# Attention heads: the division ahead of the first marking, three blocks of turned scores at the head of TensorE's round, the first scores ahead of the sample

## The reference, cut to what matters

```python
draft = jnp.einsum('bhqd,bhkd->bhqk', qr, kr)
draft = draft + jnp.where(causal_future, neg, 0.0)
_, draft_indices = jax.lax.top_k(draft, num_remain)      # the 128 largest of each row
mask = mask.at[b_idx, h_idx, s_idx, draft_indices].set(0.0)
mask = jnp.where(causal_future[None, None, :, :], neg, mask)
scores = jnp.einsum('bhqd,bhkd->bhqk', qr, kr) / np.sqrt(HD) + mask
attn = jax.nn.softmax(scores, axis=-1)
out = jnp.einsum('bhqk,bhkd->bhqd', attn, v)
```

## Time and profile before

| | |
|---|---|
| median of 3 runs | 3335.14 us (3334.58 to 3335.22) |
| the profiled execution | 3335.86 us |
| its span | 3334.0 us |
| busy share of the span: PE, DVE, ACT, POOL | 89%, 74%, 60%, 50% |
| mean granted TensorE clock over the span | 0.908 of full speed |
| the stage of the attention heads | from about 2060 to 3215 us |
| granted clock in that stage | 0.76 |

### The profile page before, as it was taken

How to read it: one execution, slowest core, us unless ns; L and a number is a source line. 1 busy time by engine, 2 the same in 40 slices (tenths; PEclk the granted TensorE clock), 3 DMA queues, 4 the chain that set the end, 5 groups by cost and what they waited for, 6 DMA issues and landing times. The chain is left out here.

```text
span 3334.0 us, 50391 instructions
## 1 busy us (share of the span) xinstructions
PE 2975.7 (89%) x15823; PEld 1814.0 (54%) x15929; DVE 2472.3 (74%) x4628; ACT 1987.7 (60%) x4218; POOL 1653.5 (50%) x3659
## 2 busy tenths in 40 slices
PE   8999999999999999999999897488888888788769
PEld 4455454464554544645545444266666666666654
DVE  5677696796876967968769767677777777777646
ACT  2463564554545645545456235888888888888723
POOL 3245264262452642634526446766666666666503
PEclk9999999999999999999999998577777777777889
DMA  2122132131221321312213100000000000000010
GB/s 91 57 87 85 69 112 89 63 111 70 86 86 70 111 90 61 111 70 86 86 57 111 56 26 2 1 1 1 2 2 1 2 1 1 1 1 1 2 49 26
DMA packets 65803, 169.62 MB, mean 51 GB/s; under 512 B 11776, under 2 KB 19328, under 8 KB 64512
## 3 DMA queue, kind: packets, MB, share of 16 engines
q1 hardware_dynamic: 54448, 115.17, 10.7%
q10 hardware_dynamic: 11088, 51.19, 4.4%
HBM read 161.08 MB, written 5.24 MB: 50 GB/s over the span
## 5 line engine op out<-in xcount | busy, mean ns | idle before, releaser
L2052 ACT ACTIVATE X<-ah_z,ah_trial 128x256 bf16<-128x256 f32 (+6 forms) x896 | 732.8, 824 | 25.2 <-POOL ah_trial L2155 14.1
L1207 ACT ACTIVATE m_mix<-m_mix,m_cs 128x128 f32<-128x128 f32 x1024 | 312.9, 388 | 256.6 <-DMA m_mix<-cs_rows 256.6
L2007 PE MATMUL ah_ps_o<-a_v,X 128*128 128x17 f32 x2304 | 353.9, 282 | 44.6 <-DVE hT L2252 44.6
L2007 PEld LDWEIGHTS ah_ps_o<-a_v,X 128*128 128x128 f32 x2304 | 338.6, 220 | 51.9 <-ACT X L2063 49.8
L2063 ACT ACTIVATE X<-ah_ps_e 128x512 f32<-128x512 f32 (+3 forms) x384 | 186.4, 486 | 192.5 <-PE ah_ps_e L1994 129.2
L2224 DVE TENSOR_SCALAR_CACHE_REDUCE X<-ah_z,ah_cut 128x256 bf16<-128x256 f32 (+6 forms) x224 | 193.7, 875 | 128.9 <-POOL ah_cut L2160 128.9
L1089 POOL TENSOR_TENSOR m_xdec<-m_xdt,m_decay_out 128x512 f32<-128x512 f32 x112 | 142.6, 1273 | 213.2 <-DVE m_xdt L1333 202.1
L1117 POOL TENSOR_TENSOR m_squares<-m_squares 128x256 f32<-128x256 f32 x128 | 107.4, 839 | 273.7 <-ACT m_squares L1219 273.7
L2237 DVE MAX8 ah_top<-ah_ps_m 128x8 f32<-128x256 f32 (+6 forms) x224 | 186.0, 830 | 69.1 <-PE ah_ps_m L1957 61.8
L1013 PE MATMUL m_ps_x<-m_w_out,m_gate 128*128 128x512 f32 x512 | 233.8, 599 | 0.0
L1013 PE MATMUL m_ps_d<-m_w_out,m_gate 128*128 128x512 f32 x512 | 233.5, 599 | 0.0
(11 more groups left out here) (319 smaller groups left out, 7782.0 us busy)
## 6 DMA issues: line engine op xcount, KB each, us to landing
m_mix<-cs_rows SPq DMA_DIRECT2D x128, 512.0 KB, 4.4
m_w_proj<-in_w_proj ACTq DMA_DIRECT2D x69, 512.0 KB, 3.3
m_fade<-fade_rows SPq DMA_DIRECT2D x224, 128.0 KB, 2.9
m_w_out<-in_w_out ACTq DMA_DIRECT2D x7, 2048.0 KB, 8.0
X<-in_x SPq DMA_DIRECT2D x8, 256.0 KB, 4.9
m_w_out<-in_w_out SPq DMA_DIRECT2D x1, 2048.0 KB, 10.1
x_away<-X SPq DMA_DIRECT2D x1, 2048.0 KB, 7.3
X<-x_away SPq DMA_DIRECT2D x8, 256.0 KB, 5.9
```

What stands on the lines that cost most here:

```text
L1207: act.activation(mix[:, u % 3, h, :], mix[:, u % 3, h, :], ACT.Relu, bias=cs[:, c, h0 + h:h0 + h + 1], scale=-1.0).then_inc(lag_done, 1)
L2007: last = pe.matmul(ps_o[:, t, :], eT[:, g % 3, b * P:(b + 1) * P], v[:, b0 + b, h // REP, :], start=i == 0 and b == 0, stop=b0 + b == t, s ...
L2052: act.activation(sign[:, at % 2, 0:(t + 1) * P], z[:, h % RING, cols(t)], ACT.Sign, bias=trial[:, h % RING, 0, t - 1:t], scale=-1.0, accum ...
```

## The change

Three things are moved, and no instruction is added or removed:

1. On PE, chunk 2 goes from behind the scores of tile 1 to the head of the round. Every later chunk but the last goes one place forward. Chunk 10, which stood between the marked scores and the scores of tile 7, now stands behind the scores of tile 6, and nothing takes its place.
2. On DVE, `divide(n - 4)` goes from behind tile 1 of the picking loop to a place ahead of `take(n - 2, 1)`.
3. On PE and DVE, the scores of tile 0 and their evacuation go ahead of the sample.

```diff
-    CHUNKS_FIRST = (0, 1)
-    CHUNKS_AFTER_MARKED = ((), (), (), (), (), (6,), (8,), (10,))
-    CHUNKS_AFTER_SCORES = ((), (2,), (3,), (4,), (5,), (7,), (9,), (11,))
+    CHUNKS_FIRST = (0, 1, 2)
+    CHUNKS_AFTER_MARKED = ((), (), (), (), (), (7,), (9,), ())
+    CHUNKS_AFTER_SCORES = ((), (3,), (4,), (5,), (6,), (8,), (10,), (11,))
@@ PE @@
                 if live(n + 1):
+                    scores(n + 1, 0)
                     sample(n + 1)
-                    scores(n + 1, 0)
@@ DVE @@
                 if live(n + 1):
+                    evacuate(n + 1, 0)
                     sample(n + 1)
-                    evacuate(n + 1, 0)
                     add_sample(n + 1)
+                if live(n - 4):
+                    divide(n - 4)
                 if live(n - 2):
                     take(n - 2, 1)
                     take(n - 2, 2)
@@
-                    if t == 1 and live(n - 4):
-                        divide(n - 4)
```

## The result

The changed kernel takes 3255.5 us (median of 4 runs, 3250.62 to 3258.75) against 3335.18 us before (4 runs). The ratio is 0.976 with a 95% interval of 0.9743 to 0.9777: 80 us less, inside the range of 3213 to 3305 and 5.5 us above the forecast of 3250. The profiled execution took 3250.62 us, with a span of 3248.7 us; it is the fastest of the four.

The account below looks back on a forecast made before the run. It took a loop of waits through ACT, POOL's cut, DVE and PE to bound the kernel. 27 rounds x (34.18 - 31.2) = 80.5 us plus 4.4 for the last three rounds gave 3250 us, range 3213 to 3305.

Parts of the forecast that it names:

- The loop before: Old round of 34.6 us: 19.95 from `take` to ACT's chunk 7, 9.44 on ACT, 5.2 through POOL's cut to `take`.
- The division in DVE's idle time: Division fits DVE's 3.44 us idle before `take`, removing PE's 1.48 us stop and 0.49 us of DVE's chain.
- The chunks: Chunks earlier on PE: chunk 7 ready 15.1 to 15.8 us after `take` instead of 19.95; ACT's waits nearly vanish.
- The new loop: DVE's chain from `take` to tile 7, then PE's head and the division: 29.9 to 32.9 us, taken as 31.2.
- Tile 0 ahead of the sample: One matmul pair on PE goes ahead of the sample's wait for ACT's `row_out`: worth 0 to 0.2 us, taken as 0.
- The clock: PE's slow stretch at the head shrinks from 10 us to some 4, the middle one stays; granted clock over 0.8.
- The sum: 27 rounds x (34.18 - 31.2) = 80.5 us, plus 4.4 for the last three rounds with picks: 85 us less.
- A full clock: First rival: PE's clock stays full once its gaps are filled, round 29.9 us, 3215 us; chance 0.12.
- Today's clock: Rival: PE's clock stays slow at the same places, round 32.9 to 33.1 us, 3300 us; chance 0.15.
- The slower side: Rival: `take` waiting for the division makes the round 35.7 us, 41 us more in all, 3376 us; chance 0.08.
- the new tie: `take` of tile 1 can't start before chunk 11 is added: 3.35 to 4.15 us behind tile 7's evacuation.
- No effect: Rival: the loop runs through another link, POOL's first move, so nothing changes, 3335 us; chance 0.03.

Follow-up runs that it names:

- warm16: The changed kernel with 16 extra matmuls in PE's gap ahead of tile 0's scores, their result overwritten: 3220.63 us.
- takes_ahead: divide_tables with the division moved behind the takes of tiles 1 and 2, ahead of the first pick: 3248.89 us.
- divide_tables: The changed kernel with the sample put back ahead of tile 0 on PE and DVE; division and chunk tables stay moved: 3243.39 us.
- divide_only: The kernel before with only the division moved ahead of the takes: 3285.49 us.
- chunk0_takes_ahead: chunk0_first with the division moved behind the takes of tiles 1 and 2: 3235.06 us.
- chunk0_first: divide_tables with chunk 0 and `add_v` of chunk 10 moved ahead of tile 0's scores on PE: 3196.96 us.

## Why the prediction was right, point by point

- **The loop before** (ACT from chunk 7, POOL's cut, DVE and PE from `take`): right, as far as its cut goes. A delay of the cut alone, by 1.0 us, made the kernel 29.5 us slower.
- **The division in DVE's idle time**: right. PE's stop of 1.48 us and 0.49 us of DVE's chain were named; alone the part brings 50 us, 1.76 us a round. The 40 us expected for it were too few.
- **The chunks**: right in kind. On top of the division the part is worth 42 us. ACT's waits fell from 5.5 to 2.2 us a round, of which the division alone had taken 2.0. I had said under 2 for the waits, and had not seen the new wait of 0.7 before `row_out`.
- **The new loop**: right. 29.63 - 2.59 - 0.49 + 0.7 for DVE gave 27.25, measured 27.0; 3.9 for the head, measured 4.2; 31.2 for the round, measured 31.40 over 26 rounds. Of the waits that came back, 0.7 in all, MAX8 of tile 2 has 0.82 in the round shown, as placed, and MAX8 of tile 1 has 0.34 that had not been seen; over the stage the two make 17.8 / 22.3 = 0.8 a round.
- **Tile 0 ahead of the sample**: the term "worth 0 to 0.2 us; I take 0" was mis-sized and had the wrong sign. It costs 12 us, 0.5 us a round. I had reasoned with the wait for ACT's `row_out` of the kernel before, though by my own sum DVE's tile 7 would be the last thing ahead of PE's head. There the sample fills the gap if it stands first, and lengthens the head if it stands second.
- **The clock**: the level was right (0.84 for the stage, over 0.80 forecast); the places weren't. I had the slow stretch at the head of the round shortened to some 4 us and the one in the middle (from 2609.75 in the earlier trace rows) left alone. It is the other way round: the middle one is gone and the one at the head stays, 6.83 us, behind the new gap of 2.0 us. 10.9 us of slow time a round were forecast; 6.8 came in the round shown, and some 7 to 8 in the mean, by a clock of 0.88 over the 26 rounds.
- **The sum**: the two divisions of the earlier trace rows bound 26 lengths of a round and not 27. Between the two profiled executions, 3335.86 and 3250.62, the 85.2 us came like this: 5.8 ahead of the first division, 26 x (34.18 - 31.40) = 72.3 in the full rounds, 6.3 from there to the last division (3077.11 to 3209.08 before, 2999.00 to 3124.64 now), where 4.4 was forecast, and 0.8 behind it. The profiled execution came out at the forecast, but it is the fastest of its four; the median is 5.5 us above.
- **Luck.** That the number is so close is in part luck. With tile 0 and the sample in the old order the kernel takes 3243.4, 6.6 us under the forecast; the swap, taken as 0, put 12 back. Two misses of opposite sign cancelled.
- **Rivals.** A full clock (3215) did not come by itself: the change opened a gap of 2.0 us while it closed two. The Trainium skill ("TensorE: Matmul & The Clock Gate", section "A second HAM failure mode: psum-queue depth-cycling") says that small, frequent gaps make the clock swing. This case agrees in part: the clock fell behind the gap of 2.00 us, but not behind those of 1.01 and 1.09, so that the reading in the prediction, that gaps of 0.8 to 1.6 us do it, is too wide. The round of 29.9 us that rival 1 put for a full clock is borne out by the one round of warm16 with a clock of 1.00, which takes 29.85. Today's clock (3300) was wrong. The slower side (3376) wanted the new tie to cost more than the change gives; the kernel got 80 us faster, and takes_ahead, without the tie, was no faster than divide_tables with it. No effect (3335) is out by the same 80 us.

## What to carry to other kernels

When several engines with in-order lists wait for each other once a round, look for the loop whose pieces add up to the length of the round, and then at once for the next longer one: an edit that is free in the old loop can be dear in the new, as the sample was. A gap in which an engine waits is worth filling with work of the next step that has its inputs already; here that took 46 us off a kernel of 3243. On PE such a gap can cost twice, by its length and by the clock behind it: the gap of 2.0 us did, those of 1.0 didn't. And a short instruction on which another engine waits is worth placing ahead of waits that it doesn't need itself: that brought 50 us in divide_only and 38 between chunk0_takes_ahead and chunk0_first, and next to nothing in takes_ahead, so the place has to be tried.

## What the runs showed of the hardware that was not expected

- 16 matmuls without use made the kernel 35 us faster: a gap of 2.0 us cut to 1.09 was enough to keep PE's clock up in some rounds, and rounds with a clock of 0.94 or more are 1.6 us shorter in the mean than those with 0.89 or less.
- Gaps of 1.0 to 1.1 us ahead of the marked scores of tiles 4 and 5, in the fast stretch, did not lower the clock in the changed kernel, though one of 0.83 us at the head of the round had gone ahead of its fall in the kernel before.
- A half-speed stretch costs far less than its length. The middle one of the earlier trace rows lasts 6.85 us; rounds of the kernel before in which it is missing or half as long are 1.1 us shorter (33.4 to 33.6 against 34.5 to 34.6).
